# Norms in a conditioned block stack: the reciprocal root on GpSimd instead of ScalarE and VectorE

## What is computed

```python
# layer 0: normalise, add a conditioned bias
mean = x.mean(-1); var = ((x - mean) ** 2).mean(-1)
out = (x - mean) * rsqrt(var + 1e-5) * weight + bias
x = (out + tanh(cond @ lin_w.T + lin_b)) * weight + bias
# layer 1: bottleneck whose weights depend on the condition (hypernetwork)
x = x + up_b @ relu(down_b @ x + bd) + bu
# layer 2: rms norm, gated gelu, quantised down projection
h = x * (scale(cond) * rsqrt(mean(x * x) + 1e-6))
val, gate = split(h @ up_w.T)
x = act_quant(val * gelu(gate)) @ weight_quant(down_w).T + x
# layer 3: attention of 16 heads and SwiGLU, each behind a conditioned rms norm
n = lambda x: gamma(cond) * x * rsqrt(mean(x * x) + 1e-6) + beta(cond)
x = x + alpha1(cond) * attention(n(x))
x = x + alpha2(cond) * (silu(n(x) @ gate.T) * (n(x) @ hidden.T) @ out_w.T + out_b)
```

## Time and profile before

| | us |
|---|---|
| median of three runs | 771.07 |
| lowest and highest | 770.39 and 772.25 |
| span of the profiled execution | 773.6 |
| busy in that span: PE / DVE / ACT / POOL | 658.1 / 431.5 / 381.9 / 55.0 |

### The profile page before, as it was taken

One profiled execution on the slowest core, in us unless ns is written; L12 is line 12 of the kernel. 1 busy time (PEld: TensorE's weight loads), 2 busy tenths in 40 slices (PEclk: granted clock), 3 DMA queues, 4 the chain that ended last, 5 costly groups with the idle time before them and its releaser, 6 DMA issues.

```text
span 773.6 us, 9912 instructions
## 1 busy us (share of the span) xinstructions
PE 658.1 (85%) x3426; PEld 436.7 (56%) x3426; DVE 431.5 (56%) x863; ACT 381.9 (49%) x729; POOL 55.0 (7%) x91
## 2 busy tenths in 40 slices
PE   2655289699989998799989998799899996999896
PEld 0411176554448876455468876354488765544585
DVE  0352078397536565588255575787165663984344
ACT  1333077426773446246863447067752554267710
POOL 4010111200000000200000000200000002000000
PEclk9755689859999999769999999689989999599999
DMA  8898521422000000502000001510000002220000
GB/s 264 292 296 285 171 87 54 95 57 44 2 1 1 1 28 28 113 13 43 2 2 1 1 28 33 118 33 11 0 0 0 14 14 62 61 44 2 1 1 28
DMA packets 34473, 44.97 MB, mean 58 GB/s; under 512 B 4736, under 2 KB 27392, under 8 KB 34304
## 3 DMA queue, kind: packets, MB, share of 16 engines
q1 hardware_dynamic: 30048, 31.87, 14.8%
q0 software_dynamic: 3872, 11.54, 5.6%
q10 hardware_dynamic: 512, 1.05, 0.4%
HBM read 28.45 MB, written 3.15 MB: 41 GB/s over the span
## 4 chain that ended last, share of the span: by engine, by line
PE 70%; DMA 11%; ACT 8%; DVE 6%; issue 2%; SPq 2%; ACTq 0%
PE psum L1071 31%; PE psum L1237 12%; PE psum L1257 8%; PE psum L1266 8%; DMA arena<-in_hyp_w 7%; DMA kst<-split 2%; PE psum L1057 2%; PE psum L1294 1%; DMA qst<-mrow_lo 1%; ACT arena L473 1%; ACT arena L613 1%; PE psum L1159 1%; PE psum L1090 1%; PE psum L1199 1%; PE psum L1144 1%
## 5 line engine op out<-in xcount | busy, mean ns | idle before, releaser
L916 DVE TENSOR_REDUCE mx<-psum 128x1 f32<-128x512 f32 x256 | 160.9, 683 | 48.8 <-PE psum L1237 48.4
L613 ACT ACTIVATE arena<-psum 128x512 f32<-128x512 f32 x256 | 140.8, 601 | 67.0 <-PE psum L1257 66.0
L1237 PE MATMUL psum<-kst,qst 96*128 96x512 f32 x192 | 102.9, 623 | 22.5 <-DMA kst<-split 20.7
L1071 PE MATMUL psum<-act,ghw_hi 128*128 128x512 f32 (+1 forms) x288 | 93.6, 394 | 0.5 <-DVE act L728 0.2
L1237 PEld LDWEIGHTS psum<-kst,qst 96*128 96x128 f32 x192 | 49.7, 261 | 72.4 <-DVE mx L916 41.1
L1257 PE MATMUL psum<-qst,kst 98*128 98x512 f32 x192 | 83.4, 454 | 3.6 <-DMA qst<-mrow_lo 1.8
L1071 PE MATMUL psum<-upw_hi,kst 128*128 128x512 f32 x256 | 72.2, 404 | 0.0
L1057 PE MATMUL psum<-arena,hblk 128*32 128x256 f32 x256 | 31.0, 579 | 44.3 <-DMA arena<-in_hyp_w 42.4
L1266 PE MATMUL psum<-arena,vals 128*17 128x512 f32 x512 | 67.4, 598 | 1.3 <-ACT arena L613 1.0
L1071 PEld LDWEIGHTS psum<-act,ghw_hi 128*128 128x128 f32 x288 | 56.7, 208 | 11.3 <-DVE act L728 1.7
L639 ACT ACTIVATE arena<-psum 128x512 f32<-128x512 f32 x32 | 19.2, 599 | 85.0 <-PE psum L1071 85.0
(11 more groups left out here) (162 smaller groups left out, 1025.2 us busy)
## 6 DMA issues: line engine op xcount, KB each, us to landing
arena<-in_hyp_w SPq DMA_DIRECT2D x32, 512.0 KB, 5.2
kst<-split POOLq DMA_DIRECT2D x44, 128.0 KB, 4.0
qst<-split SPq DMA_DIRECT2D x72, 64.0 KB, 3.4
arena<-in_x SPq DMA_DIRECT2D x4, 512.0 KB, 3.5
arena<-in_up_w POOLq DMA_DIRECT2D x8, 256.0 KB, 7.7
arena<-in_gh_w POOLq DMA_DIRECT2D x8, 256.0 KB, 3.8
out_x<-arena SPq DMA_DIRECT2D x8, 256.0 KB, 2.1
act<-split SPq DMA_DIRECT2D x24, 64.0 KB, 2.3
```

The costliest lines, as they stand in the source:

```text
L613: s.activation(probs[:, kb % 2, i, :], bank[3 + n % RING], ACT.Exp).then_inc(a_p, 1)
L916: v.reduce_max(mx[:, g % 2, col:col + 1], bank[u % RING], AX.X).then_inc(d_max, 1)
L1071: ins = pe.matmul(dst, lhs(a, c), rhs(z, c), start=start and n == 0, stop=stop and n == len(terms) - 1, skip_group_check=skip)
L1237: pe.matmul(bank[u % RING], qst[g % 3][0:KROWS, i, P * t:P * t + P], keys_of(g)[0:KROWS, i // 2, :], start=True, stop=True).then_inc(e_max, 1)
```

## The change

GpSimd computes each reciprocal root from the mean: an add of epsilon, a wait for its own add, and a power of -0.5 (a tensor operation with a constant column that is broadcast). ScalarE's `root` and `deviation` and VectorE's reciprocals behind them are gone. `square` now scales its input by 256 to the power -0.5, so the row sum is a mean. ScalarE's dummy activations that load the root's set are gone; one that loads the Exp set stands ahead of the first row of maxima, one that loads the Silu set behind `heads_turned`. GpSimd's loop over batches runs over the first three, the last stands alone, because the last has no next batch.

The core of the diff (declarations of semaphores and slots left out):

```diff
+            pool.memset(neg_half, -0.5).then_inc(pchain, 1)
...
+            def inverse_root(b, out, mean, eps, guarded, signal):
+                pool.sem_inc(keys_free, 1)
+                pool.tensor_scalar(out, mean, eps, None, ALU.add).then_inc(guarded, 1)
+                pool.wait_ge(guarded, b + 1)
+                pool.tensor_tensor(out, out, neg_half.to_broadcast(list(out.shape)), ALU.pow).then_inc(signal, 1)
+            def front_deviation(f):
+                pool.wait_ge(d_mv, f + 1)
+                inverse_root(f, stat[:, RS0, :], mv[:, :, 1], 1e-5, p_guard0, p_rs0)
+            def front_rms(f):
+                pool.wait_ge(a_ss2, f * T + T)
+                inverse_root(f, stat[:, RS2, :], stat[:, SS2, :], 1e-6, p_guard2, p_rs2)
+            def half_rms(b, h, squared, guarded, signal):
+                pool.wait_ge(squared, b * T + 2 * h + 2)
+                pair = slice(2 * h, 2 * h + 2)
+                inverse_root(b * 2 + h, stat[:, RSN, pair], stat[:, SS, pair], 1e-6, guarded, signal)
...
             for n in range(LATE):
                 load_stage(n)
+                if n == STAGES:
+                    front_deviation(0)
...
             for n in range(LATE, NSPLIT):
                 load_stage(n)
+                if n == LATE + STAGES - 1:
+                    front_rms(0)
...
                 pool.wait_ge(act_zero, b + 1)
+                for h in range(2):
+                    half_rms(b, h, a_ss3, p_guard3, p_rs3)
                 pool.wait_ge(a_qk, b * 4 + 4)
...
                 stack_k(b, 3)
+                if not last:
+                    front_deviation(b + 1)
+                for h in range(2):
+                    half_rms(b, h, a_ss4, p_guard4, p_rs4)
+                if not last:
+                    front_rms(b + 1)
...
-                    s.activation(spare[:, t, :], src[:, t, :], ACT.Square,
+                    s.activation(spare[:, t, :], src[:, t, :], ACT.Square, scale=D ** -0.5,
...
-            def root(tiles, ss, sd, rooted):
-                s.activation(stat[:, sd, tiles], stat[:, ss, tiles], ACT.Sqrt, scale=1.0 / D,
-                             bias=eps6).then_inc(rooted, 1)
-            def deviation(f):
-                s.wait_ge(d_mv, f + 1)
-                s.activation(stat[:, SD0, :], mv[:, :, 1], ACT.Sqrt, bias=eps5).then_inc(a_sd0, 1)
...
-                s.wait_ge(a_ss2, f * T + T)
-                root(slice(0, T), SS2, SD2, a_sd2)
                 s.activation(warm[:, :], eps6, ACT.Gelu)
...
-                s.activation(warm[:, :], eps6, ACT.Sqrt)
                 rounded(T - 1)
                 s.wait_ge(d_x3, b * T + 2)
                 square((0, 1), x3_tok, squares["attention"], SS, a_ss3)
-                s.wait_ge(a_ss3, b * T + 2)
-                root(slice(0, 2), SS, SDN, a_sd3)
...
+                s.activation(warm[:, :], eps6, ACT.Exp)
                 maxima_out(0)
...
-                s.activation(warm[:, :], eps6, ACT.Sqrt)
                 for h in range(2):
                     heads_turned(1, h)
-                if not last:
-                    deviation(b + 1)
+                s.activation(warm[:, :], eps6, ACT.Silu)
                 for h in range(2):
                     s.wait_ge(d_x4, b * 2 + h + 1)
                     square((2 * h, 2 * h + 1), x4_tok, squares["SwiGLU"], SS, a_ss4)
-                    s.wait_ge(a_ss4, b * T + 2 * h + 2)
-                    root(slice(2 * h, 2 * h + 2), SS, SDN, a_sd4)
...
-                v.wait_ge(a_sd0, f + 1)
-                v.reciprocal(stat[:, RS0, :], stat[:, SD0, :]).then_inc(d_rs0, 1)
...
-            def front_rms(f):
-                v.wait_ge(a_sd2, f + 1)
-                v.reciprocal(stat[:, RS2, :], stat[:, SD2, :]).then_inc(d_rs2, 1)
...
                     v.wait_ge(rooted, b * 2 + h + 1)
-                    v.reciprocal(stat[:, RSN, 2 * h:2 * h + 2], stat[:, SDN, 2 * h:2 * h + 2]).then_inc(d_rsn, 1)
-                    v.wait_ge(d_rsn, b * 4 + 2 * k + h + 1)
```

More of the change, by code:

```diff
@@ L103, in build @@
         consts = sb("consts", [P, 4])
-        eps5, eps6, magic = consts[:, 0:1], consts[:, 1:2], consts[:, 2:3]
+        eps5, eps6, magic, neg_half = [consts[:, k:k + 1] for k in range(4)]
         bn = sb("bn", [P, T, 6])
         mv = sb("mv", [P, T, 2])
-        stat = sb("stat", [P, 13, T])
-        SD0, RS0, SS2, SD2, RS2, AM, AMC, SQ, DQ, SS, SDN, RSN, AM0 = range(13)
+        stat = sb("stat", [P, 10, T])
+        RS0, SS2, RS2, AM, AMC, SQ, DQ, SS, RSN, AM0 = range(10)
         wstat = sb("wstat", [P, 4])
@@ L372, in _ @@
             pool.memset(ident16[:, :], 0.0).then_inc(pchain, 1)
-            pool.wait_ge(pchain, 2)
+            pool.wait_ge(pchain, 3)
             for m in (ident, ident16):
@@ L408, in _, with batch @@
                 load_stage(n)
+                if n == LATE + STAGES - 1:
+                    front_rms(0)
             pool.wait_ge(pool_ready, POOL_READY)
-            with pool.Fori(0, B) as b:
+            def batch(b, last):
                 pool.wait_ge(e_vg, b * 8 + 1)
@@ L424, in _ @@
                 stack_k(b, 3)
+                if not last:
[4 more added lines that the diff above has]
+                    front_rms(b + 1)
+            with pool.Fori(0, B - 1) as b:
+                batch(b, False)
+            batch(B - 1, True)
         @block.scalar
@@ L571, in batch @@
                 square((3,), x3_tok, squares["attention"], SS, a_ss3)
-                s.wait_ge(a_ss3, b * T + 4)
-                root(slice(2, 4), SS, SDN, a_sd3)
                 half_affine(b, 1, e_n1T, 1, Q_GA, Q_BA, inp[0], a_h3)
@@ L654, in _ @@
                     tanh()
-                if n == AT_STATS:
-                    deviation(0)
                 if n == AT_TURN:
@@ L885, in batch, with norm @@
                         down_out(t - 2)
-                def norm(k, h, src, xn, rooted, signal):
+                def norm(h, src, xn, rooted, signal):
                     v.wait_ge(rooted, b * 2 + h + 1)
-                    v.reciprocal(stat[:, RSN, 2 * h:2 * h + 2], stat[:, SDN, 2 * h:2 * h + 2]).then_inc(d_rsn, 1)
-                    v.wait_ge(d_rsn, b * 4 + 2 * k + h + 1)
                     for t in (2 * h, 2 * h + 1):
@@ L898, in batch @@
                 quantised(T - 1)
-                norm(0, 0, x3_tok, xn3, a_sd3, d_xn3)
+                norm(0, x3_tok, xn3, p_rs3, d_xn3)
                 down_out(T - 1)
                 lo_parts(b * 2, a_h3, inp[0], inp[1], d_h3, slice(0, HALF))
-                norm(0, 1, x3_tok, xn3, a_sd3, d_xn3)
+                norm(1, x3_tok, xn3, p_rs3, d_xn3)
                 lo_parts(b * 2 + 1, a_h3, inp[0], inp[1], d_h3, slice(HALF, L))
@@ L959, in batch @@
                 for h in range(2):
-                    norm(1, h, x4_tok, xn4, a_sd4, d_xn4)
+                    norm(h, x4_tok, xn4, p_rs4, d_xn4)
                 for h in range(2):
@@ L990, in batch @@
                             front_h2(b + 1)
-                if not last:
-                    front_rms(b + 1)
                 if last:
```

25 lines of the change are left out of this document (13 added, 12 removed).

## The result

Four runs of the changed kernel gave a median of 775.8 us, four of the kernel before 770.7 in the same session: ratio 1.0073, 95% interval 1.0051 to 1.0096. The change makes the kernel slower by 0.7%, some 5 us; 771.7 was forecast, which is within 0.2% of no change. The median lies inside the stated range of 769.0 to 776.0, at its upper end; the direction was missed. Run again beside other kernels it gave 775.99 and 1.0080 (1.0051 to 1.0109). The ratios rest on all executions and not on the medians alone, so they can differ from the medians' quotient by 0.1%. In the session of the last three kernels two of 23 executions of the kernel before took 1484 and 1997 us, and the ratios leave them out.

The account below looks back on a forecast made before the run. TensorE, with 70% of the chain, was taken to bound the kernel, so other engines' edits count only where it waits. 4 x (0 - 0.11 + 0.36) - 0.37 = +0.63 us on 771.07 gave 771.7, range 769.0 to 776.0.

Parts of the forecast that it names:

- the direction: Whole kernel: +0.63 us, the same within 0.2%; chances 40% same, 36% slower, 24% faster.
- the whole hand-over: From last sum of squares to VectorE's scaling at both norms: 0.91 us through GpSimd, bounds 0.27 and 1.65.
- The table loads that this did away with: Ahead of attention and SwiGLU norms, per batch: removing 1.48 us of ScalarE's work at each gains only 0.22 and 0.11.
- one term: GpSimd's power in the norms' chain: taken as 0.28 us from the affine select, low end 0.10, high end 0.94.

## What to carry to other kernels

Moving a short step off an engine that is busy 49% of the time to one that is busy 7% gains nothing if the step is on the path and the hand-over is longer than what it replaces: what counts is the whole hand-over, here wake, two instructions and a wait, 1.25 us against 0.55. The table loads that this did away with had been hidden but for 0.2 to 0.3 us per batch, so there was little to win; look at what is late next before you price a removed load. And where one term has no row in the trace and decides the sign, measure that instruction alone first: a series of sizes in one execution would have given it.

## What the runs showed of the hardware

- A power on GpSimd costs about 0.35 us and 0.16 us per column of 128 partitions, 10.5 us for 64 columns; an add of one column 0.17. In the kernel before ScalarE's root of two columns took 0.29 and VectorE's reciprocal 0.17.
- With 0.7 us more ahead of the transposes, TensorE's granted clock was at half speed in 15 of 20 norms, and in none of 28 without; but with the same idle time and a longer attention norm all four norms took the full-speed time. A delay of 0.69 us per half norm cost up to 11 us in all, twice its direct price of 4.9; how much of the rest is the clock's was not isolated.
- The same products took 397 or 394 ns depending on where their tiles lie, with a shift of 48 bytes per partition; a shift by 16 bytes gave the longer stretch too. What about the place decides it was not tried.
- With identical instructions the prologue, which is led by transfers, ended at 97.9 us in one execution and at 93.7 in another. A difference of two traces there says nothing below some 4 us.
